# Second FFN's table weights: GpSimd makes 12 of the 16 picks of each tile, in place of 4

## The reference, cut to what matters

```
lut      = 16 floats
gate_idx = 688 x 256 integers, 0 to 15      (up_idx the same, down_idx 256 x 688)
w        = lut[idx]
gate, up = x @ lut[gate_idx].T, x @ lut[up_idx].T
out      = (silu(gate) * up) @ lut[down_idx].T
```

## Time and profile before

| | |
|---|---|
| median of 3 runs | 926.19 us (923.75 to 926.33) |
| span of the profiled execution | 923.3 us (its own time is not listed apart from the runs; the span is 0.45 us below the lowest of them) |
| busy in the span | PE 832.7, DVE 766.5, ACT 605.9, POOL 430.6 us |
| first add of table 0 to first add of table 3 | 69.3 to 338.6 us |
| first add of table 3 to end of the last add of table 6 | 338.6 to 555.9 us |
| end of the heads | about 600 us |

### The profile page before, as it was taken

The page is one execution under the profiler, slowest core; times in us unless marked ns, Lnnn a source line. Parts: engine busy times, 40 slices in busy tenths (PEclk is TensorE's granted clock), DMA queues, the critical chain, the costliest instruction groups (busy, mean ns, idle before and its releaser), DMA issues.

```text
span 923.3 us, 13156 instructions
## 1 busy us (share of the span) xinstructions
PE 832.7 (90%) x4330; PEld 534.6 (58%) x4330; DVE 766.5 (83%) x1597; ACT 605.9 (66%) x1042; POOL 430.6 (47%) x455
## 2 busy tenths in 40 slices
PE   3889999999999999989899998679788999998997
PEld 2555665665665565655565565457555555554686
DVE  3788999889989999999899998585598687876637
ACT  5677767777777676766667767374545767657531
POOL 3134354354445277787667771171323434433301
PEclk9999999999999999999999999799989999999999
DMA  3388858966977667857857668130000000000001
GB/s 122 78 184 156 143 117 190 163 126 136 206 134 153 130 131 144 166 110 144 157 103 132 136 130 159 24 106 0 1 1 1 1 0 2 0 2 1 1 1 45
DMA packets 276867, 86.29 MB, mean 93 GB/s; under 512 B 267584, under 2 KB 272448, under 8 KB 276416
## 3 DMA queue, kind: packets, MB, share of 16 engines
q1 hardware_dynamic: 275520, 80.05, 44.8%
q0 software_dynamic: 992, 5.34, 1.9%
q10 hardware_dynamic: 288, 0.07, 0.0%
HBM read 17.29 MB, written 1.05 MB: 20 GB/s over the span
## 4 chain that ended last, share of the span: by engine, by line
PE 40%; DVE 37%; issue 9%; ACT 8%; DMA 3%; POOL 1%; SPq 1%; POOLq 0%; DVEq 0%; ACTq 0%
DVE EP L1762 9%; DVE nmax L1747 8%; PE ps L1097 7%; PE ps L1099 7%; PE ps L1098 7%; PE ps L1120 4%; DVE ptm L1861 3%; PE ps L1358 3%; PE ps L1344 3%; PE ps L1135 3%; PE ps L1323 3%; DVE ps L1947 2%; DMA ET<-EP 2%; DVE OL L1821 2%; DVE st L1661 1%
## 5 line engine op out<-in xcount | busy, mean ns | idle before, releaser
L1523 ACT ACTIVATE EP<-ps,rinv 128x1024 f16<-128x1024 f32 x128 | 142.2, 1112 | 44.5 <-DVE rinv L1757 42.9
L1762 DVE SCALAR_TENSOR_TENSOR EP<-ps,rinv,EP 128x1024 f16<-128x1024 f32 x128 | 163.3, 1276 | 2.4 <-ACT EP L1523 2.0
L1513 ACT ACTIVATE ps<-ps,nmax 128x1024 f32<-128x1024 f32 x128 | 139.2, 1088 | 35.7 <-DVE nmax L1747 35.2
L1747 DVE TENSOR_REDUCE nmax<-ps 128x1 f32<-128x1024 f32 x128 | 155.0, 1211 | 0.7 <-PE ps L1099 0.7
L1097 PE MATMUL ps<-KH,QH 128*128 128x512 f32 x256 | 115.4, 451 | 8.3 <-DVE KL L1729 4.2
L2106 POOL TENSOR_TENSOR wgu<-wgu,ptm 128x688 f32<-128x688 f32 x60 | 99.7, 1661 | 45.8 <-DVE ptm L1861 43.7
L1097 PE MATMUL ps<-ET,VH 128*128 128x512 f16 x256 | 98.7, 385 | 17.8 <-DMA ET<-EP 14.2
L1099 PE MATMUL ps<-KH,QL 128*128 128x512 f32 x256 | 100.8, 394 | 0.0
L2106 POOL TENSOR_TENSOR wdn<-wdn,ptm 128x512 f32<-128x512 f32 x45 | 57.7, 1282 | 92.2 <-DVE ptm L1861 91.0
L1098 PE MATMUL ps<-KL,QH 128*128 128x512 f32 x256 | 100.5, 392 | 0.0
L1098 PE MATMUL ps<-ET,VH 128*128 128x512 f16 x256 | 98.3, 384 | 0.0
(11 more groups left out here) (250 smaller groups left out, 2126.7 us busy)
## 6 DMA issues: line engine op xcount, KB each, us to landing
wqr<-in_wqk SPq DMA_DIRECT2D x16, 256.0 KB, 3.6
wgu<-in_tern POOLq DMA_DIRECT2D x3, 1024.0 KB, 6.1
wvr<-in_wv SPq DMA_DIRECT2D x8, 256.0 KB, 3.9
wor<-in_wo SPq DMA_DIRECT2D x16, 128.0 KB, 3.1
ET<-EP SPq DMA_TRANSPOSE x128, 4.3
X<-in_x SPq DMA_DIRECT2D x2, 512.0 KB, 5.7
prw<-in_down_idx POOLq DMA_DIRECT2D x2, 256.0 KB, 7.0
tern<-in_l_wuq_rep SPq DMA_DIRECT2D x1, 512.0 KB, 4.5
```

The lines of the kernel that those rows point to most:

```text
L1513: e.activation(bank, bank, ACT.Exp, bias=nmax[:, c:c + 1], scale=1.0, accum_out=rsum[:, c:c + 1]).then_inc(exped.sem, 1)
L1523: e.mul(EP[:, n % NE_RING, 0, :], SB(u, j), rinv[:, c:c + 1]).then_inc(e_hi.sem, 1)
L1747: e.tensor_reduce(nmax[:, c:c + 1], SB(u, j), AX.X, ALU.max, negate=True).then_inc(maxed.sem, 1)
L1762: e.scalar_tensor_tensor(out=EP[:, n % NE_RING, 1, :], in0=SB(u, j), scalar=rinv[:, c:c + 1], in1=EP[:, n % NE_RING, 0, :], op0=ALU.mult, ...
```

## The change

In each table DVE keeps the picks with v % 4 == 0 (v = 0, 4, 8, 12), and POOL makes the other twelve. DVE's picks now always write half 0 of `ptm`, POOL's always half 1; the two halves are booked apart (`free_sum[False]`, `free_sum[True]`). POOL still makes every add. The add of v = 1 waits in addition for DVE's v = 0, which an earlier pick's semaphore covered before.

```diff
--- before.py
+++ after.py
@@ -754,10 +754,10 @@
                 t, v = at
                 if v == 0 and 1 <= t < 6:
                     index_in[(t + 1) % 2].mark(t + 1)
-                (picked_g if v % 4 == 3 else picked).mark(t, v)
+                (picked if v % 4 == 0 else picked_g).mark(t, v)
                 if v > 0:
-                    SUMS[step] = free_sum[v % 2]
-                    free_sum[v % 2] = lut_added.mark(t, v)
+                    SUMS[step] = free_sum[v % 4 > 0]
+                    free_sum[v % 4 > 0] = lut_added.mark(t, v)
             elif what == "tern_wide":
                 (tern_wide_g if at[0] == 0 else tern_wide_v).mark(*at)
             elif what == "up_gate":
@@ -1845,7 +1845,7 @@
                 elif what == "lut":
                     t, v = at
                     dst, _, n = TABLES[t]
-                    if v % 4 == 3:
+                    if v % 4 > 0:
                         continue
                     w.wait_ge(*index_in[t % 2][t])
                     if v == 0:
@@ -1858,7 +1858,7 @@
                                         ALU.mult).then_inc(picked.sem, 1)
                     else:
                         w.each([SUMS[step]])
-                        e.tensor_scalar(ptm[:, v % 2, 0:n], index_tile(t), float(v), lut[:, v:v + 1], ALU.is_equal,
+                        e.tensor_scalar(ptm[:, 0, 0:n], index_tile(t), float(v), lut[:, v:v + 1], ALU.is_equal,
                                         ALU.mult).then_inc(picked.sem, 1)
                 elif what == "tern_wide" and at[0] > 0:
                     w.wait_ge(*scored[NU - 1, 3])
@@ -2094,16 +2094,15 @@
                             w.wait_ge(*lut_added[t - 1, 15])
                             e.dma_start(index_tile(t + 1), TABLES[t + 1][1]).then_inc(index_in[(t + 1) % 2].sem, 16)
                     else:
-                        if v % 4 == 3:
+                        if v % 4 > 0:
                             w.wait_ge(*index_in[t % 2][t])
                             w.wait_ge(*lut_in[0])
                             w.each([SUMS[step]])
                             e.tensor_scalar(ptm[:, 1, 0:n], index_tile(t), float(v), lut[:, v:v + 1], ALU.is_equal,
                                             ALU.mult).then_inc(picked_g.sem, 1)
-                        w.wait_ge(*(picked_g if v % 4 == 3 else picked)[t, v])
-                        if v > 1:
-                            w.wait_ge(*lut_added[t, v - 1])
-                        e.tensor_tensor(dst, dst, ptm[:, v % 2, 0:n], ALU.add).then_inc(lut_added.sem, 1)
+                        w.wait_ge(*(picked if v % 4 == 0 else picked_g)[t, v])
+                        w.wait_ge(*(lut_added[t, v - 1] if v > 1 else picked[t, 0]))
+                        e.tensor_tensor(dst, dst, ptm[:, int(v % 4 > 0), 0:n], ALU.add).then_inc(lut_added.sem, 1)
                 elif what == "tern_wide" and at[0] == 0:
                     w.wait_ge(*scored[NU - 1, 3])
                     e.tensor_copy(TU[0], tern[:, 0, :]).then_inc(tern_wide_g.sem, 1)
```

## The result

The changed kernel takes 962.27 us (median of 4 runs, 960.02 to 962.69), before it was 926.26 us (4 runs); the ratio is 1.0384, 95% interval 1.0358 to 1.0410. It is slower by 36 us. The profiled execution took 962.12 us, with a span of 960.4 us.

What follows compares the result with a forecast made beforehand. PE mostly bound the first stretch, DVE the second, where POOL would become the bound: 41.8 us too much, less 6.0 free lag and 3 gain, about 33 us on the 923.3 us span, median 959 us; range 944 to 978.

Steps and rivals of the forecast that it cites:

- second stretch: Tables 3 to 6, built without a gap from 338.6 to 555.9 us, 217.3 us long before the change.
- sum of four terms: POOL's work in tables 3 to 6: busy 166.2, gaps 3.9, new picks 82.9, their gaps 6.1; together 259.1 us.
- The channel: Tables 3 to 6: POOL's weight steps exceed their slack (squares 5.3 us, scaling 2.8 us), and PE or ACT stops.
- the stop at table 6: At v = 0 of table 6 DVE waits for table 5's last add; costs nothing by itself while POOL works on.
- Starving: POOL running out of work in tables 3 to 6; nothing in the sum, up to 10 us in the range.
- The free lag at the end: After the last add of table 6, 6.0 us of POOL's lag cost nothing.
- The first stretch: Tables 0 to 2 and weight steps, 65 to 338.6 us: 3 us of gain, with 0 and 12 as ends.
- signs of a wrong forecast: POOL's picks shorter than 2.59 us, long POOL idle times in tables 3 to 6, or a longer 65 to 338.6 us stretch.
- DVE's busy time: Whole kernel: DVE busy should fall by some 39 us, to about 728.
- The port: Tables 3 to 6: POOL's adds hold DVE's picks up, its picks do not; at worst 21 us of DVE.
- Relief: Rival: POOL keeps up and DVE's picks come off the chain until PE bounds; 912 us, chance 0.07.

Runs made afterwards that it cites:

- the narrow picks: The changed kernel with POOL's picks of tables 3 to 6 computing only 128 of 688 columns; 917.15 us, ratio 0.9906 to the kernel before.
- the even pace: The changed kernel with the first 78 steps laid three in two slots, the 64 of tables 3 to 6 two in three; 924.57 us, ratio 1.0002.
- the run without the stop: The changed kernel with v = 0 of table 6 written by POOL, so DVE does not wait there for table 5's last add; 966.83 us, ratio 1.0447.

## Why the prediction was right

The forecast was 959 us with a range of 944 to 978; it is 962.3.

**POOL's queue as the bound of the second stretch** is shown. The sum of four terms gave 259.1 us, and the stretch is 258.9 us long. The terms hold one by one: picks of 2.59 us, busy 248.2 us against 249.1 worked out, gaps 10.6 against 10.0. Cutting the picks' duration alone removes the loss (the narrow picks), and so does giving POOL the time (the even pace).

**The channel**, weight steps late by more than their slack, is shown by the waits for POOL. Each of them was named in the prediction; only the wait for `wqr`, named there too, did not occur. That the stop at table 6 costs nothing by itself is shown by the run without it.

**Starving** was rightly left at nothing: POOL waited for another engine for 0.5 us in the stretch.

**The free lag at the end** was 6.0 us in the sum; measured 7.6 us. Before, PE waited 1.22 us for DVE's `EP` between the output projection and the cast, and now it does not; that is most of the 1.6 us between.

**The first stretch** is the term that was mis-sized. I took 3 us of gain from the picks' 4.9 us on the chain. In the changed kernel POOL reaches table 3 later than before, by 1.2 us, and the run with the new split in tables 0 to 2 alone has a ratio of 0.9997. A stretch longer than today was one of my signs of a wrong forecast; but in the two runs that leave tables 0 to 2 alone and change the rest, POOL reaches table 3 at 341.2 and 341.5 us, later still, so 1.2 us is no effect that can be told. What held is the lower end that I had given, nothing. A share of the chain of 1.8% was no gain; I take it that PE's own work filled the place, as its 261 of 274 busy us let one expect.

**What lies behind the heads** was taken as unchanged. From the cast on, the changed kernel's span has 2.0 us more, 356.9 against 354.9, with the same instructions. In the traces of the eleven runs the same part takes 354.0 to 357.4 us, so this is the scatter of single executions and not the change. With these the span's growth adds up: 41.6 + 1.2 - 7.6 + 2.0 = 37.2 us, where the spans differ by 37.1 and the sum had 33. The 3 us of gain did not come, 1.2 and 2.0 us were not in the sum, and the free lag was taken 1.6 us too small. Luck had little part: these errors do not cancel, they leave 4 us, and the forecast came out near because its largest term, 41.8 us, was right.

**DVE's busy time** fell by 26.6 us, not by 39. The durations of the 56 picks fell away in full (53.3 to 14.6 us for L1861). I had added durations, but in the records each DVE instruction overlaps its neighbours by about 0.1 us, and busy time counts an overlap once: 9 us of the difference. The other 3 us are instructions that got longer: the four of L1857 in tables 3 to 6 by 1.9 us in all, and those of L1841 and L1843, which build `tern`, by 3.0, against 2 us that others lost.

**The port.** The prediction read from one row that POOL's picks do not hold DVE's up. That is so only in the middle of a POOL pick, as the last section shows. The sum did not use it, and the bound of 21 us stood well above what came: DVE's 16 picks of tables 3 to 6 took 14.5 us, 5.4 us more than 16 at 0.57.

**Relief**, the rival on the other side, was priced at 912 us and decided itself by a pick below 0.9 us. With picks of 0.72 us it came out at 917. The mechanism is real. Of its 14 us the 3 of the first stretch did not come, and of the 11.2 us in which PE stood idle in the second 9 came back. The prediction's words that nearly all of the picks' time counts there went too far: the chain held 25.4 of their 36.4 us, and the runs give a third. The measured price was decisive for the forecast. With the estimate of 1.14 us a pick, from the factor of about two in the Trainium skill, GPSIMD Engine Reference (Key points), POOL would have needed an estimated 213 of 217 us, and no loss would have been forecast.

## What to carry to other kernels

Before moving work to an idle engine, add up that engine's queue for the stretch in which the work falls, with gaps, not for the whole span: POOL at 47% of the span was at 76% of the stretch. Here the loss was the overshoot of the queue beyond the stretch, less the lag that was free at its end, to 1 us, because something urgent stood in the same queue. Below a full queue nothing could be told at loads of 84% and 88% of the stretch, and 4 to 6 us were lost at 95 and 91%, so the load alone does not say where the loss begins. A share of the chain is not a gain: 4.9 us of it gave nothing and 25.4 us of it at most 9, beside a second engine that was busy for 95% of both stretches.

## What the runs showed of the hardware

**POOL and DVE.** A DVE pick that begins while POOL executes a two-input instruction waits for its end. In the traces of all runs that is so for each of the 131 picks of 128x688 that began more than 0.21 us before that end: their records end 0.37 to 0.39 us behind it (the earlier trace rows has one). Within one of POOL's own picks of 128x688, 2.58 us and longer, it depends on the place. The 48 that began with 1.17 to 1.90 us of it to go took their plain 0.56 or 0.57 us. The 11 that began with 0.26 to 0.93 us to go ended 0.37 or 0.38 us behind it. The 9 that began 0.10 to 0.57 us behind its start took 0.63 to 1.10 us and ended 1.38 or 1.39 us before its end. (The other 12 began in its last 0.07 us or its first 0.01 us, and took the plain time.) So these POOL picks hold DVE's up early and late in their course, and not in the middle. One of the late ones is in the changed kernel, and one of the early ones in the run at even pace:

```profile
388.01 2.58 POOL L2101 TENSOR_SCALAR ptm<-wgu,lut 128x688 f32<-128x688 int32 x1
389.87 1.10 DVE L1857 TENSOR_SCALAR wgu<-prw,lut 128x688 f32<-128x688 int32 x1
...
257.16 2.58 POOL L2110 TENSOR_SCALAR ptm<-wgu,lut 128x688 f32<-128x688 int32 x1
257.26 1.09 DVE L1866 TENSOR_SCALAR wgu<-wgu,lut 128x688 f32<-128x688 int32 x1
```

The work moved to POOL cost DVE little by this: its maxima and low parts (L1747 and L1762) kept their 1.21 and 1.28 us, and the instructions named above grew by some 5 us in all.

**PE's clock.** Its granted clock was 0.93 of the upper level of 2.4 GHz in the stretch in which PE stood waiting for POOL several times, against 0.99 before. It can be seen at single waits. From 529 to 536 us PE was busy for 6.73 of 7 us at 1.00. Then it stood idle for 4.24 us (the rows under the run without the stop), and behind that:

```profile
540.00:542.00 2.00, 2.00 (x5) 0.69 (x6) 2.00 (x2) 0.92 (x1) 1.92 (x2) 0.50 0.00 0
542.00:545.00 3.00, 3.00 (x8) 1.03 (x7) 2.86 (x6) 2.54 (x5) 2.90 (x2) 0.50 0.56 108
```

That is the lower level, 1.2 GHz, and a matmul record of 0.63 us in place of 0.38. POOL's picks and adds hold 81% of the chain in the stretch and PE's three lines 3%, so I take it that this added nothing to the time; no run separates it.
